# Layer 1's mask row added by VectorE instead of TensorE, and the turned activations y made one step earlier in banks A0 and A1

## The chip, the cores and the metric

The kernel runs on one core of one Trainium2 chip. The metric is the device time of one execution in microseconds (us); of the kernel before, three executions were timed. TensorE (PE in the profile) multiplies matrices and writes PSUM; VectorE (DVE), ScalarE (ACT) and GpSimd (POOL) do the elementwise work; SyncE (SP) issues all the DMAs, in one queue, in program order. Every engine executes its own instructions in order and waits on semaphores where the program says so.

## The reference

Two transformer layers, one after the other, on x of 128 sequences x 64 tokens x 256 features, float32, 16 heads of 16, a hidden layer of 1024. The reference masks layer 1's scores by the given mask.

```
layer 0:  y = LN(x) * (1 + gamma1) + beta1        # one scale and shift per sequence
          x = x + alpha1 * (attention(y) @ proj + b)
          z = LN(x) * (1 + gamma2) + beta2
          x = x + alpha2 * (gelu(z @ fc1 + b1) @ fc2 + b2)
layer 1:  y = LN(x) * (1 + scale1) + shift1
          q, k = rotary(y @ wq + bq), rotary(y @ wk + bk);  v = y @ wv + bv
          scores = where(mask, q.k / 4, -inf);  x = x + softmax(scores) @ v @ wo + bo
          z = LN(x) * (1 + scale2) + shift2
          x = x + gelu(z @ w1 + b1) @ w2 + b2
```

## The kernel before

The tokens are cut into 16 tiles of 512 (8 sequences, four pairs g = 0 to 3 of 128 tokens). Tiles 0 to 15 are layer 0, tiles 16 to 31 the same tokens in layer 1. Every engine has a function `step(u, n, a, b, c, p)` that is written out by hand: step u does the attention of tile u (argument b, its layer), the feed-forward part of tile u-1 (c), the queries, keys and values of tile u+1 (a), the load and first normalisation of tile u+2 (n), and the last additions and the store of tile u-2 (p). Steps 2 to 12 and 18 to 29 are hardware loops, the others are written out. The order of the lines in `step` is each engine's order; nothing reorders them.

Float32 products are made of parts: each operand is split into a high part (float32r) and what is left, and TensorE makes three products of each (`product`, line 977). PSUM has eight banks: A0, A1 (scores, queries and keys), B0, B1 (turned probabilities, their product with the values, values), C (hidden layer), D0, D1 (its second product), E (turned z, heads, projection).

The scores of pair g are two units, (g, b) with b = 0 in A0 and b = 1 in A1. `scores` (L1091) makes a unit in six products. In layer 1 two more follow (L1096): `mean_w`, a matrix of 1/128, times the tile's mask row `mrow` (0 or -2^100) adds the row to all 128 rows of the bank. VectorE's `maximum` (L1444) takes the maximum per head from PSUM, and `subtract` (L1450) writes scores minus maximum to `exps` in SBUF. ScalarE's `exponential` (L804) follows, TensorE's `turn_probs` (L1110) turns the probabilities into B, ScalarE's `move_probs` (L809) copies them out, `weigh_values` (L1124) multiplies them with the values, and VectorE's `reciprocals` and `normalise_heads` (L1460, L1468) divide. `turn_heads` (L1135), `high_heads` (L815, ACT), `low_heads` (L1477, DVE) and `project` (L977 into E) make the projection; `residual` (L1493) adds it to x.

The first normalisation of tile u+2 is `first_statistics` and `first_aggregate` (DVE, L1367 and L1372, wait for the load of `x_in`), `first_rstd` (POOL, L572 to L578), `first_norm` (ACT, L738, in place in x_in) and `first_columns` (ACT, L749, the tile's scales and shifts). One step later `first_turn` (PE, L1031) turns x_in into y, pair 0 in A0 and pair 1 in B1, `y_scale` and `y_shift` (DVE, L1380 and L1387) work on it in PSUM, `first_high` (ACT, L760) and `y_low` (DVE, L1391) write its two parts to SBUF. `queries_keys(i)` for i = 0 to 3 (L977) fills A0, A1, B0, B1. In layer 0 ScalarE's `high_qk` (L776) and VectorE's `low_qk` (L1416) take them; in layer 1 VectorE's `sine` and `cosine` (L1425), four DMAs per chunk that swap partitions, GpSimd's `rotated` (L633), ScalarE's `high_qk` (L780) and GpSimd's `rotated_low` (L639).

On SyncE's queue the load of tile u+2 into x_in (L503) stands behind the store of tile u-2 (which waits for VectorE's `output`, L1517) and behind a copy of 512 KB that waits until that store has landed.

ScalarE loads a table (ACT_TABLE_LOAD) before an instruction whose function is not in the one that is loaded: before the first exponential after a gelu, and before the first gelu after an exponential.

Of the kernel before, what the change touches and what calls it, by code (L numbers as in the profile page):

```python
# [66 lines left out]
def build(nc, t, out):  # L67

    ctx = ExitStack()
    with ctx:  # L70
# [79 lines left out]
        mrow = sb("mrow", [P, TILE], F32R)  # L150
        mean_w = sb("mean_w", [P, P], F32R)
# [49 lines left out]
        pe_s, s_max, s_sub, s_exp = sem("pe_s"), sem("s_max"), sem("s_sub"), sem("s_exp")  # L201
# [71 lines left out]
        def y_bank(pair):  # L273
            return (A[0], B[1])[pair]
# [15 lines left out]

        def chunk_taken(tile, layer, i):

            return (qk_lo, upto(tile, 4, i + 1)) if layer == 0 else (rot_cosed, upto(tile - NT, 4, i + 1))
# [4 lines left out]

        NSPREAD = 16 * (NX + NJ)
# [27 lines left out]
        def _(sp):  # L327
# [140 lines left out]
            def step(u, n, a, b, c, p):  # L468
# [42 lines left out]
                if a == 1:  # L511
                    swap(u + 1, 0)
                    swap(u + 1, 1)
                    swap(u + 1, 2)
                    wait_apart(sp, sp_passed, (pe_s, upto(u + 1, 2 * G, 0)))
                    sp.dma_start(mrow[:, :].bitcast(F32), mask_tiles[u + 1 - NT].partition_broadcast(P))\
                      .then_inc(mrow_in, 16)
                    swap(u + 1, 3)
# [28 lines left out]
        def _(pool):  # L547
# [94 lines left out]
            def step(u, n, a, b, c, p):  # L642
# [40 lines left out]
                if n is not None:  # L683
# [9 lines left out]
        def _(act):  # L693
# [63 lines left out]
            def first_high(tile, pair):  # L757
                act.wait_ge(y_aff, upto(tile, 2, pair + 1))
                await_(act, pe_v, upto(tile, 2, 0))
                nc.scalar.copy(pair_of(yb[0], pair), y_bank(pair)[:, :].rearrange("p (c n) -> p c n", c=KC)).then_inc(y_hi, 1)  # L760
# [57 lines left out]
            def step(u, n, a, b, c, p):  # L818
# [40 lines left out]
                if a is not None:  # L859
# [3 lines left out]
                if a is not None:  # L863
# [28 lines left out]
                elif known(u) and u == 0:  # L892
                    high_piece(2, 0, 2)
                if a == 1:
# [59 lines left out]
                if known(u) and u == NT - 2:  # L954
                    act.wait_ge(mod_done, 32)
                if n is not None:
                    first_norm(u + 2)
                    first_columns(u + 2, n)
                if known(u) and u == 0:
# [10 lines left out]
        def _(pe):  # L970
# [32 lines left out]
            def gate_products():  # L1003
# [3 lines left out]
                pe.wait_ge(consts_ready, 2)  # L1007
# [39 lines left out]
            def queries_keys(tile, layer, i, attn):  # L1047
# [6 lines left out]
                elif attn is None:  # L1054
                    pass
                elif i == 1:
                    pe.wait_ge(s_sub, upto(tile - 1, 2 * G, 6))
# [19 lines left out]
            def scores(u, layer, g, b, a):  # L1077
                if b == 0:
                    pe.wait_ge(spread_in[g % 2], upto(u, 2 * NSPREAD, (g // 2 + 1) * NSPREAD))
                    if layer == 1 and g == 0:  # L1080
                        pe.wait_ge(mrow_in, upto(u - NT, 16, 16))
                await_(pe, s_sub, upto(u, 2 * G, 2 * g + b - 1))
# [4 lines left out]
                s = slice((2 * g + b) * S, (2 * g + b + 1) * S)  # L1087
                for c in range(KC):
                    dst = A[b][:, c * 256:(c + 1) * 256]
                    for p, q in BY_WEIGHTS:  # L1090
                        ins = nc.tensor.matmul(dst, qpad[g % 2][:, c, p, b, :, :].rearrange("p x s -> p (x s)"),  # L1091
                                               kpad[g % 2][:, c, q, :, b * S:(b + 1) * S], start=(p, q) == (0, 0),
                                               stop=layer == 0 and (p, q) == BY_WEIGHTS[-1])
# [80 lines left out]
            def step(u, n, a, b, c, p):  # L1174
# [31 lines left out]
                if a is not None:  # L1206
# [18 lines left out]
                if a is not None:  # L1225
# [512 lines left out]
```

## Time and profile before

| What | Before |
|---|---|
| three executions | 1841.35 us median, 1840.35 to 1844.5 |
| profiled execution | 1841.5 us, its span 1839.7 us (from first to last instruction) |
| PE busy over the span | 1784.3 us, 97% |
| DVE, ACT, POOL busy | 1247.0, 1230.2, 852.7 us (68%, 67%, 46%) |
| mean granted TensorE clock | 0.992 of 2.4 GHz |
| a step of layer 0 (472.22 to 527.07) | 54.85 us, PE busy 54.24 |
| a step of layer 1 (1366.25 to 1421.64) | 55.39 us, PE busy 55.20 |

Busy time is the union of an engine's instructions. Successive products overlap in the records, so that the time one costs is the distance of its start from the next one's, not its length. A step is taken from the first score product of one tile to that of the next. All times in rows are us from the start of the span.

### The profile page before, as it was taken

To read this page: it belongs to the slowest core of one execution; us is meant where nothing else is said; L and a number is where in the kernel's file an instruction comes from. 1 tells how busy PE (TensorE), PEld (TensorE's weight loads), DVE (VectorE), ACT (ScalarE), POOL (GpSimd) and SP (SyncE) were. 2 spreads that over 40 slices of the span, in tenths; PEclk is the share of its full clock that TensorE was granted. 3 is DMA by queue.
4 is the path that set the end of the run, shared out by engine and by line. 5 is a ranking of instruction groups with operands and counts; after the bars stand their busy time and mean duration, and the time that the engine had idled before them with its cause. 6 is when DMAs were issued, how large, how long until landed. Compare 5 with 4: busy or idle time off the path is not lost.

```text
span 1839.7 us, 41543 instructions
## 1 busy us (share of the span) xinstructions
PE 1784.3 (97%) x12623; PEld 1634.3 (89%) x12623; DVE 1247.0 (68%) x2985; ACT 1230.2 (67%) x2265; POOL 852.7 (46%) x1036
## 2 busy tenths in 40 slices
PE   7799999999999999999999999999999999999998
PEld 6688999888989888999888999999999999999986
DVE  6777676667676667677677766776766776666751
ACT  4466767766776766677657767666767667767663
POOL 2233433333433433433635566555566555566544
PEclk9899999999999999999999999999999999999999
DMA  6545545444544435554453332333332334342320
GB/s 166 144 113 127 126 91 126 105 111 125 128 99 116 113 104 130 127 140 103 116 152 100 91 107 88 105 102 105 89 109 86 107 99 107 82 114 88 96 72 35
DMA packets 330283, 199.93 MB, mean 109 GB/s; under 512 B 160995, under 2 KB 314597, under 8 KB 330213
## 3 DMA queue, kind: packets, MB, share of 16 engines
q1 hardware_dynamic: 330212, 199.06, 41.0%
q8 instruction: 36, 0.59, 0.1%
q14 instruction: 35, 0.28, 0.1%
HBM read 80.98 MB, written 17.33 MB: 53 GB/s over the span
## 4 chain that ended last, share of the span: by engine, by line
PE 74%; DVE 11%; issue 7%; ACT 2%; SPq 2%; POOL 2%; DMA 1%; DVEq 0%; POOLq 0%; ACTq 0%
PE C L977 17%; PE D L1168 16%; PE B L977 9%; PE B L1124 8%; PE A L1091 6%; PE B L1110 4%; PE A L977 4%; PE E L977 4%; DVE mx L1444 3%; PE A L1096 2%; DVE o_sb L1468 1%; DVE exps L1450 1%; PE E L1135 1%; PE E L1043 1%; DVE z_lo L1391 1%
## 5 line engine op out<-in xcount | busy, mean ns | idle before, releaser
L593 POOL TENSOR_TENSOR h_lo<-hact,h_hi 128x512 fp32r<-128x512 f32 x256 | 331.0, 1293 | 234.9 <-ACT h_hi L800 219.8
L1168 PE MATMUL D<-wgt_hi,h_hi 128*128 128x256 f32 x1024 | 263.4, 290 | 0.0
L1091 PE MATMUL A<-k_pad,q_pad 128*128 128x256 f32 x1536 | 256.1, 293 | 5.7 <-DMA q_pad<-q_flat 2.8
L809 ACT COPY probs_turned<-B 128x512 f32<-128x512 f32 x256 | 149.3, 584 | 167.6 <-PE B L1110 167.5
L1168 PE MATMUL D<-wgt_lo,h_hi 128*128 128x256 f32 x1024 | 255.6, 282 | 0.0
L1124 PE MATMUL B<-v_blocks,probs_turned 128*128 128x68 f32 x2048 | 254.3, 271 | 1.3 <-ACT probs_turned L809 1.3
L1124 PEld LDWEIGHTS B<-v_blocks,probs_turned 128*128 128x128 f32 x2048 | 248.7, 192 | 6.5 <-ACT probs_turned L809 2.3
L795 ACT ACTIVATE hact<-C,b_col 128x512 f32<-128x512 f32 x256 | 175.9, 687 | 83.6 <-PE C L977 81.2
L1444 DVE TENSOR_REDUCE mx<-A 128x8 f32<-128x512 f32 x256 | 174.4, 681 | 68.8 <-PE A L1096 41.2
L1091 PEld LDWEIGHTS A<-k_pad,q_pad 128*128 128x128 f32 x1536 | 211.3, 191 | 9.8 <-DMA q_pad<-q_flat 3.5
L804 ACT ACTIVATE exps<-exps 128x512 f32<-128x512 f32 x256 | 161.6, 632 | 84.7 <-DVE exps L1450 82.3
L1168 PEld LDWEIGHTS D<-wgt_lo,h_hi 128*128 128x128 f32 x1024 | 195.3, 191 | 1.4
L1168 PEld LDWEIGHTS D<-wgt_hi,h_hi 128*128 128x128 f32 x1024 | 194.6, 190 | 2.0 <-ACT h_hi L800 0.4
L583 POOL TENSOR_SCALAR rs<-mv 128x1 f32<-128x1 f32 x128 | 28.7, 224 | 360.9 <-DVE mv L1501 352.0
L1450 DVE TENSOR_TENSOR exps<-A,mx 128x512 f32<-128x512 f32 x256 | 176.1, 688 | 5.9 <-PE B L1110 0.4
L977 PE MATMUL C<-z_hi,wgt_hi 128*128 128x512 f32 x512 | 169.0, 411 | 5.0 <-ACT hact L795 4.5
L1168 PE MATMUL D<-wgt_hi,h_lo 128*128 128x256 f32 x1024 | 166.8, 285 | 4.7 <-POOL h_lo L593 4.5
L1110 PE MATMUL B<-ident,exps 128*128 128x128 f32 x1024 | 155.8, 275 | 7.4 <-DVE rotation L1425 2.7
L800 ACT CAST h_hi<-hact 128x512 fp32r<-128x512 f32 x256 | 159.1, 621 | 4.2
L1468 DVE TENSOR_TENSOR o_sb<-B,rden 64x128 f32<-64x128 f32 x512 | 146.7, 287 | 20.6
L977 PE MATMUL C<-z_hi,wgt_lo 128*128 128x512 f32 x512 | 159.8, 393 | 0.0
L977 PE MATMUL C<-z_lo,wgt_hi 128*128 128x512 f32 x512 | 158.9, 391 | 0.0
(141 smaller groups left out, 3874.5 us busy)
## 6 DMA issues: line engine op xcount, KB each, us to landing
k_pad<-k_flat SPq DMA_DIRECT2D x512, 64.0 KB, 2.1
q_pad<-q_flat SPq DMA_DIRECT2D x256, 128.0 KB, 2.4
gates<-gates SPq DMA_DIRECT2D x64, 256.0 KB, 4.5
x_bias<-x_bias SPq DMA_DIRECT2D x32, 512.0 KB, 3.3
rotation<-rotation SPq DMA_DIRECT2D x256, 64.0 KB, 1.9
x_in<-in_x SPq DMA_DIRECT2D x16, 512.0 KB, 4.5
gates<-gated_bias SPq DMA_DIRECT2D x32, 256.0 KB, 4.7
x_res<-in_x SPq DMA_DIRECT2D x16, 512.0 KB, 4.8
```

The lines of the kernel that those rows point to most:

```text
L593: pool.tensor_tensor(hb[1][:, m % 2, :], hact[:, m % 2, :], hb[0][:, m % 2, :].bitcast(F32), ALU.subtract).then_inc(h_lo, 1)
L795: nc.scalar.activation(hact[:, m % 2, :], C[:, :], ACT.Gelu, bias=b1_col[:, layer, m:m + 1]).then_inc(gelu, 1)
L800: nc.scalar.copy(hb[0][:, m % 2, :], hact[:, m % 2, :]).then_inc(h_hi, 1)
L804: nc.scalar.activation(exps[:, b, :], exps[:, b, :], ACT.Exp, scale=SCORE_SCALE).then_inc(s_exp, 1)
L977: ins = nc.tensor.matmul(dst, l[p], r[q], start=(p, q) == order[0] and n == 0, stop=(p, q) == order[-1] and n == len(pairs) - 1)
L1091: ins = nc.tensor.matmul(dst, qpad[g % 2][:, c, p, b, :, :].rearrange("p x s -> p (x s)"), kpad[g % 2][:, c, q, :, b * S:(b + 1) * S], sta ...
L1110: ins = nc.tensor.transpose(B[b][:, n * P:(n + 1) * P], exps[:, b, n * P:(n + 1) * P], ident[:, :])
L1124: ins = nc.tensor.matmul(B[b][:, n * 68:(n + 1) * 68], pt[:, b, n * P:(n + 1) * P], moving, start=True, stop=True)
L1168: ins = nc.tensor.matmul(Dk[g // 2][:, (g % 2) * D:(g % 2 + 1) * D], hb[p][:, m % 2, g * P:(g + 1) * P], w_slice(q, W_FF2, D, m, 0, D), st ...
L1444: nc.vector.tensor_reduce(mx[:, b, :], A[b][:, :].rearrange("p (h k) -> p h k", k=S), AX.X, ALU.max)\
L1450: nc.vector.tensor_tensor(exps[:, b, :].rearrange("p (h k) -> p h k", k=S), A[b][:, :].rearrange("p (h k) -> p h k", k=S), mx[:, b, :].rea ...
L1468: ins = nc.vector.tensor_tensor(o_sb[p, b, :].rearrange("p (n j d) -> p n j d", n=4, j=2), sums_of(b)[p, :, x, :, 0:HD], rden[p, b, :].rea ...
```

## The change

Layer 1's `scores` ends with the six products; `mean_w` is gone, and `mrow` is plain float32. VectorE gets a new instruction per unit, `mask`: it reads the bank and the mask row and writes the sum to `exps`. `maximum` then reads `exps`, and `subtract` reads and writes `exps`, so that TensorE may fill the bank again after `mask` (`scores_taken`) and not after `subtract`. Layer 0's units are as before.

From step 1 on, y of tile u+2 is turned at the end of step u, behind `turn_probs(u, 3, 1)`, into A0 and A1; `y_scale`, `y_shift`, `first_high` and `y_low` move to the end of the step too, and the next step's first scores wait for `y_low`. `queries_keys(u+1, 0)` moves up to where the turns were. For that, `first_statistics`, `first_aggregate`, `first_rstd`, `first_norm` and `first_columns` move up in the step. SyncE's order stays as it was.

```diff
+            def mask(u, g, b):
+                s = slice((2 * g + b) * S, (2 * g + b + 1) * S)
+                dve.wait_ge(pe_s, upto(u, 2 * G, 2 * g + b + 1))
+                await_(dve, pe_pt, upto(u, 2 * G, 2 * g + b - 1))
+                if b == 0:
+                    dve.wait_ge(mrow_in, upto(u - NT, 16, 16))
+                nc.vector.tensor_tensor(by_head(exps[:, b, :]), by_head(A[b][:, :]),
+                                        mrow[:, s].rearrange("p (o s) -> p o s", o=1).to_broadcast([P, 8, S]),
+                                        ALU.add).then_inc(s_masked, 1)
+
+            def maximum(u, layer, g, b):
+                if layer == 1 and g in MASKED:
+                    mask(u, g, b)
+                    dve.wait_ge(s_masked, upto(u - NT, NMASK, masked_units(g, b)))
+                    src = exps[:, b, :]
...
+                nc.vector.tensor_reduce(mx[:, b, :], by_head(src), AX.X, ALU.max).then_inc(s_max, 1)
...
+            def subtract(u, layer, g, b):
                 dve.wait_ge(s_max, upto(u, 2 * G, 2 * g + b + 1))
+                src = exps[:, b, :] if layer == 1 and g in MASKED else A[b][:, :]
...
             def scores(u, layer, g, b, a):
...
-                await_(pe, s_sub, upto(u, 2 * G, 2 * g + b - 1))
+                if g > 0:
+                    pe.wait_ge(*scores_taken(u, layer, g - 1, b))
...
+                if g == 0 and a is not None and not y_soon(u):
+                    pe.wait_ge(y_lo, upto(u + 1, 2, b + 1))
...
-                    if layer == 1:
-                        row = mrow[:, s].rearrange("p (o s) -> p o s", o=1).to_broadcast([P, NJ, S])
-                        ins = nc.tensor.matmul(dst, mean_w[:, :], row, start=False, stop=True)
...
@@ TensorE's step
-                if a is not None:
+                if a is not None and y_soon(u):
                     first_turn(u + 1, 0, b)
                     first_turn(u + 1, 1, b)
+                elif a is not None:
+                    queries_keys(u + 1, a, 0, b)
...
                     turn_probs(u, 3, 1, a)
+                if n is not None and b is not None:
+                    first_turn(u + 2, 0, n)
+                    first_turn(u + 2, 1, n)
...
@@ ScalarE's step, behind hidden_high(u - 1, 3)
+                if n is not None and b is not None and a == 0:
+                    first_norm(u + 2)
+                    first_columns(u + 2, n)
...
@@ ScalarE's step, behind exponential(u, 3, 1)
+                if n is not None and b is not None and a == 1:
+                    first_norm(u + 2)
+                    first_columns(u + 2, n)
...
@@ VectorE's step
+                if n is not None and b is not None:
+                    first_statistics(u + 2)
                 if a == 0:
                     low_qk(u + 1, 0)
...
+                if n is not None and b is not None and a == 0:
+                    first_aggregate(u + 2)
                 if a == 0:
                     low_qk(u + 1, 1)
```

VectorE at the start of a step of layer 1 (the loop of steps 18 to 29), before. E is the bank of the turned z, A0 and A1 hold the scores:

```order
L1444 TENSOR_REDUCE mx<-A0 128x8
L1380 TENSOR_TENSOR E<-E,mod_tile 128x512
L1450 TENSOR_TENSOR exps<-A0,mx 128x512
L1444 TENSOR_REDUCE mx<-A1 128x8
L1387 TENSOR_TENSOR E<-E,mod_tile 128x512
L1450 TENSOR_TENSOR exps<-A1,mx 128x512
```

The same place now:

```order
L1483 TENSOR_TENSOR exps<-A0,mrow 128x512
L1495 TENSOR_REDUCE mx<-exps 128x8
L1412 TENSOR_TENSOR E<-E,mod_tile 128x512
L1502 TENSOR_TENSOR exps<-exps,mx 128x512
L1483 TENSOR_TENSOR exps<-A1,mrow 128x512
L1495 TENSOR_REDUCE mx<-exps 128x8
L1419 TENSOR_TENSOR E<-E,mod_tile 128x512
L1502 TENSOR_TENSOR exps<-exps,mx 128x512
```

Each unit has one instruction more, and the pieces of z stand between as before.

ScalarE in the middle of a step of layer 0 (the loop of steps 2 to 12), before; h_hi is the hidden layer's high part, exps the unit (3, 0), q_flat chunk 2 of tile u+1:

```order
L800 CAST h_hi<-hact 128x512
L804 ACT_TABLE_LOAD
L804 ACTIVATE exps<-exps 128x512
L776 ACTIVATE q_flat<-B0,qk_bias 128x4x128
L815 ACTIVATE ot_hi<-E,v_bias 128x128 x2
```

The same place now:

```order
L818 CAST h_hi<-hact 128x512
L756 ACTIVATE x_in<-x_in,nb1,rs1 128x256 x4
L767 COPY mod_tile<-mod 128x32
L822 ACT_TABLE_LOAD
L822 ACTIVATE exps<-exps 128x512
```

The normalisation of tile u+2 now stands ahead of the table load and of the exponential of (3, 0).

VectorE in the middle of a step of layer 1, before; A0 and A1 hold chunks 0 and 1 of tile u+1's keys, B0 the weighed values of unit (2, 0):

```order
L1501 BN_AGGR mv2<-st2 128x2
L1425 SCALAR_TENSOR_TENSOR rotation<-A0,qk_bias,rtab 128x512
L1425 SCALAR_TENSOR_TENSOR rotation<-A0,qk_bias,rtab 128x512
L1425 SCALAR_TENSOR_TENSOR rotation<-A1,qk_bias,rtab 128x512 x2
L1460 RECIPROCAL rden<-B0 128x8
```

The same place now:

```order
L1552 BN_AGGR mv2<-st2 128x2
L1399 BN_STATS st1<-x_in 128x6 x4
L1457 SCALAR_TENSOR_TENSOR rotation<-A0,qk_bias,rtab 128x512
L1457 SCALAR_TENSOR_TENSOR rotation<-A0,qk_bias,rtab 128x512
L1404 BN_AGGR mv1<-st1 128x2 x4
L1457 SCALAR_TENSOR_TENSOR rotation<-A1,qk_bias,rtab 128x512 x2
L1511 RECIPROCAL rden<-B0 128x8
```

The statistics of x_in, which wait for its load, now stand ahead of the first chunk's rotation; they stood some twenty instructions later.

## Rows read from the trace of the kernel before

**Rows 1.** Busy us of PE, PEld, DVE, ACT, POOL, clock, DMA by stretch.

```profile
1366.25:1421.64 55.39, 55.20 (x401) 51.37 (x400) 38.01 (x90) 37.96 (x72) 31.77 (x39) 1.00 0.35 99
1366.25:1384.20 17.95, 17.95 (x151) 17.54 (x150) 15.99 (x34) 12.22 (x23) 8.11 (x8) 1.00 0.35 88
```

**Rows 2.** TensorE's timeline, unit (2, 1): start us, us, engine line op, [idle before].

```profile
1379.44 0.28 PE L1096 MATMUL A<-mrow,mean_w 128*128 128x256 f32 x1
1379.56 0.51 PE L1091 MATMUL A<-k_pad,q_pad 128*128 128x256 f32 x3
```

**Rows 3.** VectorE's timeline, unit (2, 1) and low_heads(0), same step.

```profile
1380.28 0.68 DVE L1444 TENSOR_REDUCE mx<-A 128x8 f32<-128x512 f32 x1
1380.99 0.69 DVE L1450 TENSOR_TENSOR exps<-A,mx 128x512 f32<-128x512 f32 x1
1381.60 0.60 DVE L1477 SCALAR_TENSOR_TENSOR ot_lo<-E,v_bias,ot_hi 128x128 fp32r<-128x128 f32 x2
```

**Rows 4.** TensorE's timeline, project(0) and the turns of y, same step.

```profile
1382.52 0.40 PE L977 MATMUL E<-wgt_hi,ot_hi 128*128 128x256 f32 x2
...
1383.24 0.60 PE L1031 MATMUL A<-ident,x_in 128*128 128x128 f32 x4
1383.78 0.63 PE L1031 MATMUL B<-ident,x_in 128*128 128x128 f32 x4
```

**Rows 5.** Instructions of line L1305: ns min/median/max, first and last start.

```profile
L1305 DVE TENSOR_TENSOR wgt_lo<-gates,wgt_hi x4: 685/686/715, 969.6 to 1004.3; 128x512 fp32r<-128x512 f32 x4
```

**Rows 6.** VectorE's timeline at 965 us, two subtractions between SBUF tensors.

```profile
965.32 3.28 DVE L1305 TENSOR_TENSOR wgt_lo<-w_raw,wgt_hi 128x512 fp32r<-128x512 f32 x2
```

**Rows 7.** Load of x_in, layer 1 step: SyncE's timeline; us to landing.

```profile
1390.81 0.39 SPq L503 DMA_DIRECT2D x_in<-mid  x1
...
x_in<-mid SPq DMA_DIRECT2D x1, 512.0 KB, 4.1
```

**Rows 8.** Timelines of DVE, ACT and PE, same step: chunk 0, turn_probs(3, 0).

```profile
1392.86 1.41 DVE L1425 SCALAR_TENSOR_TENSOR rotation<-A,qk_bias,rtab 128x512 f32<-128x512 f32 x2 [1.41 <-PE A L977]
...
1398.90 0.62 ACT L780 CAST k_flat<-rotation 128x512 fp32r<-128x512 f32 x1 [1.30 <-POOL rotation L633]
...
1404.43 0.60 PE L1110 MATMUL B<-ident,exps 128*128 128x128 f32 x4
```

**Rows 9.** Load of x_in, layer 0 step: SyncE's timeline; us to landing.

```profile
496.93 0.39 SPq L503 DMA_DIRECT2D x_in<-in_x  x1
...
x_in<-in_x SPq DMA_DIRECT2D x1, 512.0 KB, 4.7
```

**Rows 10.** Timelines of DVE and POOL, layer 0 step: statistics and rstd of x_in.

```profile
515.31 1.37 DVE L1367 BATCH_NORM_STATS2 st<-x_in 128x6 f32<-128x256 f32 x4
516.95 0.38 DVE L1372 BATCH_NORM_AGGREGATE mv<-st 128x2 f32<-128x6 f32 x4 [0.27 <-DVE st L1367]
...
518.42 0.23 POOL L572 TENSOR_SCALAR rs<-mv 128x4 f32<-128x4 f32 x1
...
520.26 0.24 POOL L578 TENSOR_SCALAR nb<-nb 128x4 f32<-128x4 f32 x1 [0.20 <-POOL nb L576]
```

**Rows 11.** Groups by line, whole span: xcount | busy us, mean ns | idle before.

```profile
L738 ACT ACTIVATE x_in<-x_in,nb,rs 128x256 f32<-128x256 f32 x128 | 66.4, 590 | 9.1 <-POOL nb L578 9.1
```

**Rows 12.** Timelines of ACT, DVE and PE, layer 0 step: up to turn_probs(3, 0).

```profile
503.70 1.28 ACT L804 ACT_TABLE_LOAD   x1
507.85 0.63 ACT L804 ACTIVATE exps<-exps 128x512 f32<-128x512 f32 x1 [2.87 <-DVE exps L1450]
...
509.09 0.75 DVE L1416 SCALAR_TENSOR_TENSOR q_flat<-B,qk_bias,q_flat 128x512 fp32r<-128x512 f32 x1 [1.27 <-ACT q_flat L776]
...
509.98 0.65 PE L1110 MATMUL B<-ident,exps 128*128 128x128 f32 x4
```

**Rows 13.** Columns as in rows 1 (the clock last but two), at a long wait.

```profile
951.40:954.80 3.40, 1.18 (x8) 0.78 (x7) 0.75 (x1) 1.89 (x2) 3.28 (x3) 1.00 0.10 36
954.80:961.60 6.80, 5.47 (x21) 4.92 (x21) 4.28 (x8) 5.20 (x10) 4.20 (x4) 0.50 0.17 59
```

More of the change, by code:

```diff
@@ L271, in qk_bank, with y_soon, y_bank @@
             return (A + B)[i]
-        def y_bank(pair):
-            return (A[0], B[1])[pair]
+        def y_soon(u):
+            return known(u) and u < 1
+        def y_bank(tile, pair):
+            return (A[0], B[1] if known(tile) and tile < 2 else A[1])[pair]
         def pair_of(buf, pair):
@@ L289, in head_rows, with masked_units, scores_taken @@
             return E[:, 0:2 * P].rearrange("p (b x q) -> p b x q", b=2, x=NX)[:, :, x, :]
+        def masked_units(g, b):
+            return 2 * sum(m < g for m in MASKED) + (b + 1 if g in MASKED else 0)
+        def scores_taken(tile, layer, g, b):
+            if layer == 1 and g in MASKED:
+                return s_masked, upto(tile - NT, NMASK, masked_units(g, b))
+            return s_sub, upto(tile, 2 * G, 2 * g + b + 1)
         def chunk_taken(tile, layer, i):
@@ L682, in step @@
                     rotated_low(u + 1, 3)
-                if n is not None:
+                if n is not None and b is None:
                     first_rstd(u + 2)
@@ L862, in step @@
                     second_norm(u, 0)
[L863 removed]
+                if y_soon(u):
                     first_high(u + 1, 1)
@@ L1224, in step @@
                     modulations(Dk[0], ada_raw[0][:, :, D:2 * D], ada_raw[0][:, :, 0:D])
-                if a is not None:
+                if a is not None and y_soon(u):
                     queries_keys(u + 1, a, 0, b)
@@ L1587, in step @@
                     gate_heads(u, 1)
-                if a is not None:
+                if y_soon(u):
                     y_shift(u + 1, 1)
@@ L1593, in step @@
                     residual(u, b, 1)
-                if a is not None:
+                if y_soon(u):
                     y_low(u + 1, 0)
@@ L1620, in step @@
                     low_piece(3, 0, 3)
+                if n is not None and b is not None:
+                    first_statistics(u + 2)
                 if a == 0:
@@ L1631, in step @@
                     cosine(u + 1, 0)
+                if n is not None and b is not None and a == 1:
+                    first_aggregate(u + 2)
+                if a == 1:
                     sine(u + 1, 1)
@@ L1665, in step @@
                     second_aggregate(u, 2)
-                if n is not None:
+                if n is not None and b is None:
                     first_statistics(u + 2)
                     first_aggregate(u + 2)
+                elif n is not None:
+                    for pair in range(2):
+                        y_scale(u + 2, pair)
+                        y_shift(u + 2, pair)
                 if known(u) and u == NT - 2:
@@ L1694, in step @@
                     second_aggregate(u, 3)
+                if n is not None and b is not None:
+                    y_low(u + 2, 0)
+                    y_low(u + 2, 1)
                 if known(u) and u == NT - 1:
```

108 lines of the change are left out of this document (57 added, 51 removed).

## The prediction

> **What bounds it now.** The busy times of the whole span put TensorE at 97% (the table above). I then looked at single steps. A step of layer 1 takes 55.39 us and TensorE is busy in 55.20 of them [rows 1]: it hardly waits, so a us of work taken from it is a us gained, and a us of new waiting is a us lost, since the rest of its step has no holes to make it up. The second row cuts off the part up to turn_heads(1): there VectorE is busy 15.99 of 17.95 us, and 38.01 - 15.99 = 22.0 in the 37.4 us behind it. So VectorE, at 69% over the step, is nearly full in one part of it, and the change puts six of its eight new instructions there. The third view is the timeline, engine by engine, around the places where something is moved.
>
> **What TensorE sheds.** One mask product starts at 1379.44 and the next score product at 1379.56 [rows 2]: 0.12 us. Two per unit, 8 units, 16 tiles make 256, or 30.7 us.
>
> **What VectorE takes on.** No row shows a mask addition. The nearest are the maximum and the subtraction of the same 128x512: 0.68 and 0.69 us, 0.71 from start to start where the second needs the first, 0.61 where the next does not [rows 3]. The maximum needs the mask, so I take 0.71 of the two. Reading SBUF instead of PSUM gains nothing for the maximum and the subtraction: a 128x512 subtraction between SBUF tensors takes 0.686 us [rows 5], against 0.69 [rows 3]. The Trainium skill's page "VectorE: DVE Perf Modes", section "The TRN2 errata", counts 58 cycles beside the elements for an SBUF source and 120 for a PSUM source, which would be an estimated 0.065 us less for each of the twelve before project(0), 0.8 us a step; the trace does not agree with it ([rows 3, 5]), and the sum goes by the rows.
>
> Another price is a collision. Two subtractions with both inputs in SBUF took 3.28 us together [rows 6] instead of 1.37 [rows 5], 0.96 more each, while GpSimd worked beside them. The new subtraction has both inputs in SBUF (exps and mx); the old one had one in PSUM and took 0.69. For each subtraction the bounds are 0 (mx has only 8 elements a row) and 0.96. GpSimd is busy 8.11 of the first 17.95 us, in 8 instructions [rows 1], which I expect mostly at the start of the step: I take one collision of 0.55, near the middle; bounds 0 and 6 x 0.96 = 5.8. The Trainium skill's page "SBUF — State Buffer", section "Who interferes with whom", says that a VectorE instruction with two SBUF inputs and a GpSimd instruction that reads SBUF exclude each other for the whole instruction. The trace agrees for two full inputs [rows 6]; that an input as small as mx is enough, no row here shows.
>
> **Where it ends first: project(0).** Six units stand ahead of low_heads(0) on VectorE: 6 x 0.71 = 4.26, less 0.24 because the first scores are two products sooner, plus 0.55: 4.6. low_heads(0) ended at 1381.60 + 0.60 = 1382.2 [rows 3] and would end at 1386.8. project(0), which needs it, started at 1382.52 [rows 4]: 4.3 late (3.7 without the collision), where TensorE by itself would come 6 x 0.24 = 1.4 early. What is queued behind it on TensorE's queue is all the rest of the step.
>
> **The load of x_in, layer 1.** The change moves the statistics of tile u+2 far up VectorE's order but leaves the load where it was, behind the store of tile u-2 and a copy. It is issued at 1390.81 and lands 4.1 later [rows 7], at 1394.9. The store waits for VectorE's output behind low_heads(1), which the 4.3 us shift: 1399.2. VectorE now waits there ahead of chunk 0's rotation, which started at 1392.86 [rows 8]. Statistics 1.37 [rows 10]: the rotation starts at 1400.6. From its start to the end of ScalarE's cast of the chunk it is 1398.90 + 0.62 - 1392.86 = 6.66 us [rows 8] (sine, four DMAs, GpSimd): 1407.2. On ScalarE a table load of 1.28 and the exponential of (3, 0), 0.63, follow [rows 12]: 1409.1, and then turn_probs(3, 0), which was at 1404.43 [rows 8]: 4.7 late. Behind it come the turns of y, now at the end of the step: two groups 0.54 apart [rows 4], 1.1 us. The last unit's mask and a collision of its subtraction stand ahead of low_heads(2) and project(2): between 0 and 1.2, I take 0.6. A step is 4.7 + 1.1 + 0.6 = 6.4 longer; steps 16 to 29, 14 x 6.4 = 90. Steps 30 and 31 load no x_in; there the 4.3 are lessened by the products behind project(0) and, in step 30, by the turns of y: 3.0 and 3.8, 7 in all.
>
> **The same in layer 0.** No masks here, but x_in is issued at 496.93 and lands 4.7 later [rows 9], 501.6. Statistics 1.37, low_qk(0) 0.75 [rows 10, 12], aggregates 0.38: 504.1. GpSimd's rstd, 520.26 + 0.24 - 518.42 = 2.08 [rows 10]: 506.2. Four normalisations, 66.4 / 32 = 2.08 [rows 11]: 508.3. The table load was over at 504.98, in 2.87 us of idle time that hid it [rows 12]; the order has it behind the normalisations now, 1.28: 509.6. So the exponential of (3, 0) starts 1.75 after 507.85, and with it high_qk(2), low_qk(2) and turn_probs(3, 0), which was at 509.98 right behind low_qk(2) (509.09 + 0.75) [rows 12]. TensorE's turns of y are gone ahead of this place, but a chain that starts with a DMA sets it, so they are gained nowhere and cost 1.1 behind it. 2.85 a step; 15 steps (1 to 15) make 42.
>
> **TensorE's clock.** Around 951 TensorE was busy 1.18 of 3.40 us, and the next 6.8 us were granted 0.50 [rows 13], 1.2 GHz, which loses 3.4 us of work. The new waits are of that size (about 5.7 us before project(0), in several pieces; 2 to 3 before turn_probs(3, 0)). Bounds: none, and 3.4 in each of 29 steps, 99. As the waits come in pieces between work I take one step in six: 16.
>
> **At nothing.** The next step's scores wait for y_low at the end of the step; TensorE's back(5) and hidden(7) stand there and should cover it. Without that cover it would be one more 0.7 instruction a step, 20 us. The mask row's load waits for the last mask now, ahead of swap 3 on SyncE's queue; swap 3 waits for a later instruction of VectorE's anyway.
>
> **Sum.** The shorter products are within the lines above. 42 + 90 + 7 + 16 = 155 us on the profiled execution's 1841.5, which stands at the median of 1841.35: 1996 us.
>
> **Rivals.** (1) Ends on the other side: the masks are hidden and TensorE's 30.7 us come through: 1811. For it, TensorE's full row [rows 1]; against it, project(0) had 0.3 us of room (1382.2 to 1382.52) and 4.6 come in. It decides at an addition of 0.05 us a unit. Chance 0.03. (2) x_in lands in time and only the masks tell: 4.3 less the 0.5 of the last units' products, 3.8 in 16 steps: 1902. It needs a landing ahead of about 500 in layer 0, that is a load issued 2 us sooner; the waits ahead of it on SyncE's queue are not changed, but a shorter transfer is possible. 0.15. (3) The masks fit better than I think (VectorE slips into waits), x_in is late: layer 0's 42 alone, since in layer 1 a chain that starts 1.4 us earlier gives back what the turns of y cost: 1884. 0.06. (4) The clock falls in every step, and collisions add to it: 1980 + 99 = 2079, half of it 2030. For it [rows 13] and the length of the waits; 0.17. My forecast has 0.58; 0.01 is left for no change.
>
> **Range.** The likeliest case by itself: 1950 to 2030 (x_in half a us earlier or later moves all 29 steps, 15 us; collisions 0 or 1 us more in 14 steps, the clock 0 to 50). To hold 8 in 10 it must reach (2) and a good part of (4): 1885 to 2060. A change under 0.2%, 3.7 us, could not be told from none by these runs. Slower by more 0.96, within 0.01, faster 0.03.
>
> **What would show it.** Steps of layer 0 near 57.7 us, with an ACT_TABLE_LOAD between the normalisation of x_in and the exponential, and VectorE idle some 6 us ahead of L1399 with the DMA as releaser. Steps of layer 1 near 62 us; project(0) waiting some 2 us for VectorE's ot_lo, more pieces of waiting for ScalarE's exponentials and copies before it; VectorE's first rotation behind the statistics. Subtractions (L1502) of up to 1.6 us beside GpSimd. The granted clock below 0.99. Wrong would be: layer 0 steps of 55 us (x_in came sooner, or something else was ready later), or a layer 1 step under 58.

## The result, and the profile after

The changed kernel takes 2043.88 us (median of 6 executions, 2032.9 to 2051.47) against 1842.81 us of the kernel before, run beside it (6 executions, 1840.35 to 1844.5): a ratio of 1.1088, 95% interval 1.1065 to 1.1111, so 11% slower. The prediction had 1996 us; the loss is about 201 us where 155 were forecast. The profiled execution took 2038.69 us, its span 2036.8.

The head of its page:

```profile
span 2036.8 us, 41383 instructions
...
PE 1822.0 (89%) x12367; PEld 1638.4 (80%) x12367; DVE 1381.8 (68%) x3112; ACT 1243.1 (61%) x2265; POOL 872.2 (43%) x1036
```

TensorE was full before (97%) and now has 11% of holes; its busy time is even 38 us longer than before although 256 products are gone; the granted clock is lower (0.971 after 0.992). Stretch by stretch, with the columns of [rows 1]: a step of layer 1, its part up to turn_heads(1), a step of layer 0, two more of layer 0, and step 0:

```profile
1494.35:1558.68 64.33, 55.24 (x386) 49.46 (x384) 46.13 (x99) 38.46 (x70) 33.21 (x38) 1.00 0.30 86
1494.35:1517.29 22.94, 18.30 (x138) 16.46 (x136) 20.64 (x41) 12.81 (x20) 8.96 (x7) 1.00 0.27 69
...
383.36:442.37 59.01, 55.74 (x386) 50.51 (x384) 38.12 (x93) 38.59 (x70) 20.76 (x27) 0.97 0.43 107
442.37:499.99 57.62, 54.42 (x385) 49.33 (x384) 38.12 (x93) 38.63 (x70) 20.77 (x27) 1.00 0.43 109
...
32.66:94.77 62.11, 42.79 (x273) 38.84 (x273) 44.04 (x116) 29.55 (x62) 8.37 (x17) 0.89 0.53 135
```

Against [rows 1]: the layer 1 step went from 55.39 to 64.33 us, and its first part from 17.95 to 22.94, of which VectorE is busy 20.64. A step of layer 0 takes 57.6 us at a granted clock of 1.00 (54.85 before), 59.0 where the clock fell for a while (0.97), and step 0, which holds no feed-forward work, grew from 54.2 to 62.1.

Where TensorE waits in that layer 1 step (its timeline; the last column is the idle time ahead of the row and who ended it):

```profile
1499.56 0.66 PE L1138 MATMUL B<-ident,exps 128*128 128x128 f32 x4 [1.04 <-ACT exps L822]
1502.09 0.66 PE L1138 MATMUL B<-ident,exps 128*128 128x128 f32 x4 [1.15 <-ACT exps L822]
1506.88 0.65 PE L1138 MATMUL B<-ident,exps 128*128 128x128 f32 x4 [0.39 <-DVE o_sb L1519]
1515.11 0.47 PE L1004 MATMUL E<-wgt_hi,ot_hi 128*128 128x256 f32 x2 [2.06 <-DVE ot_lo L1528]
1533.03 0.73 PE L1004 MATMUL B<-y_hi,wgt_hi 128*128 128x512 f32 x2 [1.10 <-DVE o_sb L1519]
1539.04 0.65 PE L1138 MATMUL B<-ident,exps 128*128 128x128 f32 x4 [1.80 <-DVE rotation L1457]
1542.58 0.47 PE L1004 MATMUL E<-wgt_hi,ot_hi 128*128 128x256 f32 x2 [1.49 <-DVE ot_lo L1528]
```

The first four are the delay ahead of project(0), in pieces (4.6 us of idle time), which now starts 20.76 us into the step and not 16.27 [rows 4]. The other three (4.4 us) come behind the late x_in in the step; two of them have a second cause, which the experiments below show. On VectorE in the same step:

```profile
1497.39 1.46 DVE L1502 TENSOR_TENSOR exps<-exps,mx 128x512 f32<-128x512 f32 x1
1498.77 0.68 DVE L1483 TENSOR_TENSOR exps<-A,mrow 128x512 f32<-128x512 f32 x1
...
1527.87 1.41 DVE L1399 BATCH_NORM_STATS2 st<-x_in 128x6 f32<-128x256 f32 x4 [6.11 <-DMA x_in<-mid]
1529.19 1.39 DVE L1457 SCALAR_TENSOR_TENSOR rotation<-A,qk_bias,rtab 128x512 f32<-128x512 f32 x2
...
1535.38 1.61 DVE L1502 TENSOR_TENSOR exps<-exps,mx 128x512 f32<-128x512 f32 x1
1536.92 0.74 DVE L1457 SCALAR_TENSOR_TENSOR rotation<-B,qk_bias,rtab 128x512 f32<-128x512 f32 x1
1538.16 0.75 DVE L1457 SCALAR_TENSOR_TENSOR rotation<-B,qk_bias,rtab 128x512 f32<-128x512 f32 x1 [0.51 <-POOL k_flat L655]
...
1540.26 1.65 DVE L1502 TENSOR_TENSOR exps<-exps,mx 128x512 f32<-128x512 f32 x1
```

and on GpSimd beside them:

```profile
1495.90 2.40 POOL L624 TENSOR_TENSOR x_bias<-x_res,b_bc 128x1024 f32<-128x1024 f32 x1
...
1535.16 1.29 POOL L609 TENSOR_TENSOR h_lo<-hact,h_hi 128x512 fp32r<-128x512 f32 x1
1536.41 1.72 POOL L655 TENSOR_TENSOR k_flat<-rotation,k_flat 128x512 fp32r<-128x512 f32 x1
...
1540.08 1.29 POOL L655 TENSOR_TENSOR k_flat<-rotation,k_flat 128x512 fp32r<-128x512 f32 x1 [0.73 <-ACT k_flat L798]
```

Two things are to be seen. VectorE stands idle for 6.11 us until x_in lands, with chunk 0's rotation right behind the statistics. And three subtractions take 1.46, 1.61 and 1.65 us: each ends 0.54 to 0.55 us after the GpSimd instruction that was running when it began (1495.90 + 2.40 = 1498.30, and 1497.39 + 1.46 = 1498.85; likewise 1536.45 and 1536.99, 1541.37 and 1541.91). In turn the GpSimd instruction that starts under a subtraction is stretched, to 1.72 us in place of 1.29. The mask at 1498.77, which takes one input from PSUM, runs beside GpSimd in its 0.68.

The load (SyncE's timeline, then us to landing), which answers to [rows 7]:

```profile
1523.85 0.39 SPq L519 DMA_DIRECT2D x_in<-mid  x1
...
x_in<-mid SPq DMA_DIRECT2D x1, 512.0 KB, 4.0
```

Issued 29.50 us into the step, 24.56 before. In the layer 0 step that begins at 499.99, on VectorE, ScalarE and TensorE:

```profile
529.64 1.41 DVE L1399 BATCH_NORM_STATS2 st<-x_in 128x6 f32<-128x256 f32 x4 [6.80 <-DMA x_in<-in_x]
...
534.37 2.08 ACT L756 ACTIVATE x_in<-x_in,nb,rs 128x256 f32<-128x256 f32 x4 [4.49 <-POOL nb L594]
536.58 1.28 ACT L822 ACT_TABLE_LOAD   x1
537.87 0.63 ACT L822 ACTIVATE exps<-exps 128x512 f32<-128x512 f32 x1
...
539.99 0.65 PE L1138 MATMUL B<-ident,exps 128*128 128x128 f32 x4 [2.47 <-DVE q_flat L1448]
```

This step takes 57.97 us. It shows the chain that was forecast: landing, statistics, rstd, four normalisations, a table load that nothing hides any more, exponential, and turn_probs(3, 0) behind it, 40.00 us into the step and not 37.76 [rows 12].

### The profile page after: what moved, and what is told of

Same layout as the page of the kernel before. It is cut to its first block, busy times and chain, and to the rows that moved or that the text cites. A ratio compares the mean times of both kernels' runs of the same rounds, so it can differ in the third digit from the quotient of the medians.

```text
span 2036.8 us, 41383 instructions
## 1 busy us (share of the span) xinstructions
PE 1822.0 (89%) x12367; PEld 1638.4 (80%) x12367; DVE 1381.8 (68%) x3112; ACT 1243.1 (61%) x2265; POOL 872.2 (43%) x1036
## 4 chain that ended last, share of the span: by engine, by line
PE 36%; DVE 27%; issue 15%; DMA 12%; POOL 4%; ACT 3%; SPq 3%; DVEq 1%; POOLq 0%; ACTq 0%
PE C L1004 10%; PE B L1004 6%; PE D L1196 6%; DVE mx L1495 5%; DVE exps L1502 4%; DMA x_in<-in_x 4%; PE E L1004 3%; PE B L1152 3%; DVE exps L1483 3%; DMA x_in<-mid 3%; DMA mid<-x_bias 3%; DVE o_sb L1519 2%; DVE ot_lo L1528 2%; DMA out<-x_bias 2%; PE B L1138 2%
## 5 line engine op out<-in xcount | busy, mean ns | idle before, releaser
L609 POOL TENSOR_TENSOR h_lo<-hact,h_hi 128x512 fp32r<-128x512 f32 x256 | 339.6, 1326 | 281.0 <-ACT h_hi L818 270.9
L1196 PE MATMUL D<-wgt_hi,h_hi 128*128 128x256 f32 x1024 | 269.8, 295 | 0.0
L1152 PE MATMUL B<-v_blocks,probs_turned 128*128 128x68 f32 x2048 | 263.1, 277 | 1.5 <-ACT probs_turned L827 1.5
L1152 PEld LDWEIGHTS B<-v_blocks,probs_turned 128*128 128x128 f32 x2048 | 254.2, 197 | 11.1 <-ACT probs_turned L827 5.3
L1196 PE MATMUL D<-wgt_lo,h_hi 128*128 128x256 f32 x1024 | 261.1, 287 | 0.0
L1122 PE MATMUL A<-k_pad,q_pad 128*128 128x256 f32 x1536 | 245.7, 297 | 12.8 <-DVE k_flat L1448 4.3
L1138 PE MATMUL B<-ident,exps 128*128 128x128 f32 x1024 | 161.9, 282 | 91.3 <-ACT exps L822 36.3
L1122 PEld LDWEIGHTS A<-k_pad,q_pad 128*128 128x128 f32 x1536 | 205.5, 194 | 19.3 <-issue 9.9
L1138 PEld LDWEIGHTS B<-ident,exps 128*128 128x128 f32 x1024 | 121.0, 145 | 120.1 <-issue 71.1
L1399 DVE BATCH_NORM_STATS2 st<-x_in 128x6 f32<-128x256 f32 x128 | 45.0, 413 | 188.3 <-DMA x_in<-mid 99.9
```

Source lines behind the costliest of these rows:

```text
L609: pool.tensor_tensor(hb[1][:, m % 2, :], hact[:, m % 2, :], hb[0][:, m % 2, :].bitcast(F32), ALU.subtract).then_inc(h_lo, 1)
L1138: ins = nc.tensor.transpose(B[b][:, n * P:(n + 1) * P], exps[:, b, n * P:(n + 1) * P], ident[:, :])
L1152: ins = nc.tensor.matmul(B[b][:, n * 68:(n + 1) * 68], pt[:, b, n * P:(n + 1) * P], moving, start=True, stop=True)
L1196: ins = nc.tensor.matmul(Dk[g // 2][:, (g % 2) * D:(g % 2 + 1) * D], hb[p][:, m % 2, g * P:(g + 1) * P], w_slice(q, W_FF2, D, m, 0, D), st ...
```

## The experiments

The theory after the result: x_in, still loaded where it was, holds VectorE up in every step; in layer 1 the masks delay project(0), and the subtraction in SBUF collides with GpSimd. The rivals: that x_in is a bystander, that ScalarE's new order sets layer 0, that the masks would fit by themselves. Every kernel is given against the kernel before, run on the same chip; in brackets stand the ratio of the two and its 95% interval. Differences between experiments are differences of medians, some of them from two chips; on these chips the kernel before took 1841.84 to 1843.01 us.

**x_in sooner.** The load stands behind the spreads of group 3:

```diff
                     spread_queries(u, 3)
+                if n is not None and x_soon(u, b):
+                    wait_apart(sp, sp_passed, (pe_yt, upto(u + 1, 2, 2)))
...
+                    sp.dma_start(x_in, tokens_of(u + 2, n)).then_inc(x_loaded, 16)
```

> Against the changed kernel, only the load of x_in is moved: from behind the store of tile u-2 and the copy to right behind the spreads of group 3 of the same step. My theory: the landing of x_in sets the middle of every step. Then VectorE's 6.1 us of idle time ahead of the statistics is gone, layer 0 steps go from about 57.5 us to 54.9 to 55.8, and layer 1 steps from 64.5 to 60 to 62 (project(0) still comes 4.8 late), so about 40 + 14 x 3.5 = 90 us less than the changed kernel's 2044: 1955 (1935 to 1980). Rival: the load is a bystander, the masks and collisions in layer 1 and the normalisation and table load on ScalarE in layer 0 set the steps anyway; then at most 0.5 us a step is gained: over 2025.

Measured: 1939.71 us (1.0521, 1.0489 to 1.0553), 104 us less than the changed kernel. One step of either layer (columns of rows 1):

```profile
474.47:528.77 54.30, 54.11 (x385) 49.22 (x384) 38.39 (x93) 38.64 (x70) 20.78 (x27) 1.00 0.48 116
1411.24:1472.63 61.39, 56.06 (x386) 50.87 (x384) 45.63 (x99) 38.39 (x70) 32.14 (x38) 0.97 0.31 90
```

The time lies in the range given, and the load does set both layers: layer 0 loses all of its 2.75 us and 0.5 more, layer 1 loses 3 of its 9. In layer 1 TensorE still waits 0.87 us for turn_probs(3, 0) and 0.78 us for project(2) (1.80 and 1.49 in the changed kernel), and for project(0). What remains there is due to the masks, as the next experiments show.

**The same, with x_in's normalisation later on ScalarE** (x_in_norm_later: in layer 0 behind the exponential of (3, 1) too).

```diff
-                if n is not None and b is not None and a == 0:
-                    first_norm(u + 2)
-                    first_columns(u + 2, n)
...
-                if n is not None and b is not None and a == 1:
+                if n is not None and b is not None:
                     first_norm(u + 2)
```

> As x_in_sooner, and in layer 0 the four normalisations of x_in on ScalarE stand behind the exponential of (3, 1), as they do in layer 1, so that the table load ahead of the exponential of (3, 0) has its idle time back. My theory: with x_in in time the normalisations come early enough either way, so the same time as x_in_sooner within 8 us, layer 0 steps near 55.0 us. Rival: ScalarE's order was the cause in layer 0 (2.75 us a step); then this run is 30 to 45 us faster than x_in_sooner.

Measured: 1951.35 us (1.0584, 1.0562 to 1.0607), 12 us slower than x_in sooner, where its expectation allowed 8; layer 0 steps of 54.83 against 54.30. Layer 1 is the same program in both. A step of each layer:

```profile
480.05:534.88 54.83, 54.37 (x386) 49.19 (x384) 38.51 (x93) 38.28 (x70) 20.77 (x27) 1.00 0.47 115
1485.93:1547.03 61.10, 54.78 (x385) 49.33 (x384) 45.37 (x99) 38.45 (x70) 32.64 (x38) 1.00 0.32 90
```

The rival (30 to 45 us faster) falls: ScalarE's order is no burden when x_in is in time, and the place that the change chose is the better one. About half of the 0.5 us stands in the trace: TensorE waits 0.27 us for VectorE's q_flat ahead of turn_probs(3, 1), a wait that x_in sooner does not have. The rest was not followed up.

**The normalisation later, x_in late.** The same edit in the changed kernel itself.

> The changed kernel with x_in's load as late as there, but in layer 0 the four normalisations of x_in on ScalarE stand behind the exponential of (3, 1) instead of ahead of the table load and the exponential of (3, 0). My theory, by the prediction's chain in layer 0: landing, statistics, aggregates, rstd, normalisations 2.08, table load 1.28, exponential, high_qk(2), low_qk(2), turn_probs(3, 0); without the normalisations and the table load in it the exponential is in time and layer 0 steps fall from about 57.5 to 58.5 us to 55 to 56: 2044 - 30 = 2014 (2005 to 2025), layer 1 as in the changed kernel. Rival: the late statistics hold VectorE up by themselves (low_qk(0) and all behind it) and the normalisations lie in ScalarE's waits: layer 0 steps of 57 and more, 2035 to 2050.

Measured: 2022.15 us (1.0974, 1.0951 to 1.0997), 22 us less than the changed kernel and in the range given; a layer 0 step, a little longer than the 55 to 56 us expected, and the row of turn_probs(3, 0) in it:

```profile
493.21:549.50 56.29, 54.71 (x386) 49.31 (x385) 38.25 (x93) 38.32 (x70) 20.82 (x27) 1.00 0.45 112
```

```profile
531.02 0.65 PE L1135 MATMUL B<-ident,exps 128*128 128x128 f32 x4 [0.46 <-DVE q_flat L1445]
```

The wait fell from 2.47 to 0.46: the normalisations and the exposed table load were part of the chain, as the prediction had it, and about half of layer 0's loss (1.3 us of 2.75 by these rows, 22 / 15 = 1.5 on average). The other half, 1.4 us against the kernel before, remains with the statistics still late; with the same order on ScalarE and the load in time a step took 54.83 us (x_in_norm_later). So both halves come from the one late load.

**y alone.** The mask products are back on TensorE (`MASKED = ()`, `mean_w` as before), y stays one step sooner.

> The changed kernel with the mask products back on TensorE and no mask on VectorE in any unit; y stays one step sooner. My theory: layer 0 as in the changed kernel (about 57.5 to 58.5 us a step, 50 us in all); in layer 1 project(0) is in time, x_in lands as before about 29 us into the step, the statistics hold chunk 0's rotation up by 3.7 us, of which 1.7 were slack: steps of 57.5 to 59.5. In all 1842 + 50 + 14 x 3 = 1934 (1915 to 1955). Rival: the move of y costs in layer 0 only, and layer 1 is slow by the masks alone: layer 1 steps of 55.4 to 56, 1892.

Measured: 1918.2 us (1.0408, 1.039 to 1.0425), in the range given; steps of 57.83 in layer 0 and 57.63 in layer 1, so that y costs in both layers and the rival falls:

```profile
497.18:555.01 57.83, 54.48 (x385) 49.37 (x384) 38.13 (x93) 38.65 (x70) 20.79 (x27) 1.00 0.44 109
1430.36:1487.99 57.63, 55.41 (x401) 51.19 (x400) 38.30 (x91) 38.18 (x70) 31.73 (x38) 1.00 0.33 96
```

**The masks alone.** y, x_in and the statistics as before.

> The kernel before with the masks on VectorE and no mask products, and y, x_in and their statistics where they stood before. Layer 0 is the kernel before, 54.8 us a step. My theory: project(0) waits 4.8 us longer for low_heads(0), the masks and the long subtractions of (3, 0) and (3, 1) add 1 to 2: layer 1 steps of 59.5 to 61.5, 1842 + 16 x 5.1 = 1924 (1905 to 1945). Rival: the masks are mostly hidden when nothing else is moved, and the late x_in made layer 1 slow: layer 1 steps of 54 to 56.5, 1820 to 1860.

Measured: 1948.42 us (1.0579, 1.0559 to 1.0599), 3 us above the range given. A layer 1 step, and project(0) in it:

```profile
1417.57:1478.68 61.11, 54.96 (x386) 49.38 (x384) 44.72 (x98) 38.31 (x71) 32.68 (x39) 1.00 0.31 90
```

```profile
1438.54 0.47 PE L1004 MATMUL E<-wgt_hi,ot_hi 128*128 128x256 f32 x2 [2.05 <-DVE ot_lo L1528]
```

The masks cost 105 us and y 75, together 181 of the 201. The rest fits with the two lengthening each other's chain: the masks shift the store that x_in's load waits for, and y hangs on that load, which is issued 24.94 us into a layer 1 step with y alone and 29.50 with both. That this makes the whole 20 us is not shown. Masks that would be hidden if nothing else moved fall as a theory.

**The masks in PSUM.** From x_in sooner, without the collision: the sum is written back to the bank, and maximum and subtraction read the bank again.

```diff
-                nc.vector.tensor_tensor(by_head(exps[:, b, :]), by_head(A[b][:, :]),
+                nc.vector.tensor_tensor(by_head(A[b][:, :]), by_head(A[b][:, :]),
                                         mrow[:, s]...
...
-                src = exps[:, b, :] if layer == 1 and g in MASKED else A[b][:, :]
+                src = A[b][:, :]
```

> As x_in_sooner, but VectorE adds the mask row in place in PSUM: maximum and subtraction read the PSUM bank again, so no subtraction has both inputs in SBUF; the bank is released at the subtraction instead of at the mask. My theory: in x_in_sooner's trace a subtraction that runs beside GpSimd ends 0.54 us after GpSimd's instruction does, and takes 1.46, 1.48 and 0.94 us in place of 0.69 (units (0, 0), (3, 0), (3, 1)); here all take 0.69 and no GpSimd instruction is stretched to 1.73; project(0) waits 0.6 us less and turn_probs(3, 0) and project(2) lose most of their 0.87 and 0.78 us of waiting: layer 1 steps of 59.2 to 60.2 instead of 61.4, 1939 - 14 x 1.7 = 1915 (1905 to 1923). Rival: the masks' own 0.7 us each set the steps and the collisions lie in waits: within 8 us of x_in_sooner; or the later release makes the next scores wait and it is slower than x_in_sooner.

Measured: 1914.99 us (1.041, 1.0391 to 1.043), 24.7 us less than x_in sooner by the medians (20 by the two ratios). The subtractions, ns min/median/max: first the changed kernel's two forms, then this kernel's:

```profile
L1502 DVE TENSOR_TENSOR exps<-A,mx x128: 678/691/694, 35.0 to 950.2; 128x512 f32<-128x512 f32 x128
L1502 DVE TENSOR_TENSOR exps<-exps,mx x128: 680/692/2377, 970.5 to 1984.1; 128x512 f32<-128x512 f32 x128
```

```profile
L1506 DVE TENSOR_TENSOR exps<-A,mx x256: 675/691/693, 34.9 to 1855.8; 128x512 f32<-128x512 f32 x128
```

A layer 1 step at a granted clock of 1.00, to be held against the 61.10 above:

```profile
1336.54:1395.84 59.30, 54.77 (x385) 49.38 (x384) 43.64 (x99) 38.48 (x70) 31.67 (x38) 1.00 0.32 93
```

With one input in PSUM none takes more than 0.693 us; with both in SBUF the longest took 2.377. In this step no GpSimd addition or subtraction of 128x512 takes more than 1.30 us, turn_probs(3, 0) no longer waits, and project(2) waits 0.55. So the collision is shown, and it costs 20 to 25 us in 16 steps, 1.3 to 1.5 each (1.8 by the two rows at a granted 1.00). This is a net price: the bank now comes free only at the subtraction, and the next scores wait for it in places (0.25 and 1.12 us in this step). project(0) waits all the same (2.09 us; steps of 59.3 to 60.9): that is the masks' own time.

**x_in sooner and y, no masks on VectorE.** x_in sooner with `MASKED = ()`.

> As x_in_sooner with the mask products back on TensorE and no mask on VectorE: y one step sooner and the load of x_in in time. My theory: layer 0 as in x_in_sooner (54.3 us a step); in layer 1 the waits that y_alone still has (0.89 and 1.33 us) go with the late x_in: TensorE full, 54.6 to 55.2 us a step against 55.4; step 0 still some 6 us over. In all 1842 - 8 - 7 + 6 = 1833 (1825 to 1845), faster than the kernel before by 0 to 1 per cent. Rival: layer 1's rotation chain is late by the statistics ahead of it in any case: 56 to 57.5 us a step, 1850 to 1870.

Measured: 1829.11 us (0.9931, 0.9914 to 0.9947), in the range given and faster than the kernel before by 0.7%:

```profile
473.18:527.50 54.32, 54.18 (x385) 49.28 (x384) 38.38 (x93) 38.64 (x70) 20.75 (x27) 1.00 0.48 116
1357.48:1412.42 54.94, 54.94 (x402) 51.25 (x400) 38.43 (x91) 38.16 (x70) 31.69 (x38) 1.00 0.35 100
```

Both layers gain half a us a step. In layer 0 part of it is a wait of the kernel before (TensorE's timeline, turn_heads(1), which waited behind the turns of y for VectorE's residual); with the longer queries_keys(0) in the turns' place it is covered:

```profile
490.09 0.44 PE L1135 MATMUL E<-ident,o_sb 128*128 128x128 f32 x2 [0.29 <-DVE x_res L1493]
```

**The last mask on VectorE.** As x_in_y with `MASKED = (3,)`, in SBUF and, in a second kernel, in PSUM.

> As x_in_y, but VectorE adds the mask for group 3 alone (two units a step, in SBUF as in the changed kernel), TensorE multiplies it for groups 0 to 2. My theory: ahead of project(0) VectorE is full, so masks cost there what they take; behind it, where the statistics no longer wait, it has room, and the mask of group 3 costs only its collisions with GpSimd (0.8 and 0.25 us): layer 1 steps of 54.8 to 56, 1828 to 1850. Rival: a mask costs its 0.7 us at any place: 56 us or more a step, 1850 to 1865.

> As mask_last, with the mask added in place in PSUM. My theory: no collision is left and the two masks fit: 0.48 us a step less on TensorE than x_in_y, 54.2 to 54.8 us a step in layer 1, 4 to 8 us faster than x_in_y and 5 to 15 faster than mask_last: 1820 to 1835. Rival: as for mask_last, the same time as mask_last within 3 us.

Measured: 1854.32 us in SBUF (1.0066, 1.0049 to 1.0083) and 1839.66 us in PSUM (0.9987, 0.9977 to 0.9997), both above the ranges given (1828 to 1850, 1820 to 1835). In SBUF, TensorE waits in a step for turn_probs(3, 0) and project(2):

```profile
1410.33 0.65 PE L1154 MATMUL B<-ident,exps 128*128 128x128 f32 x4 [0.86 <-DVE rotation L1474]
1413.15 0.47 PE L1013 MATMUL E<-wgt_hi,ot_hi 128*128 128x256 f32 x2 [0.78 <-DVE ot_lo L1545]
```

and in PSUM for project(2) alone:

```profile
1400.55 0.47 PE L1011 MATMUL E<-wgt_hi,ot_hi 128*128 128x256 f32 x2 [0.54 <-DVE ot_lo L1541]
```

The collision costs 14.7 us here too. It is part of why the SBUF kernel came out where its rival had put it (1850 to 1865). But the expectation that two masks fit behind project(0) was wrong as well: in PSUM they still cost 10.6 us against x_in_y, and low_heads(2) stands behind them.

**low_heads(2) first**, and a kernel that also moves the last modulations of step 0 behind y_low.

```diff
+                if b == 1:
+                    low_heads(u, b, 2)
                 if b is not None:
                     maximum(u, b, 3, 1)
                     subtract(u, b, 3, 1)
+                if b == 0:
                     low_heads(u, b, 2)
```

> As mask_last_psum, and in layer 1 low_heads(2) stands ahead of the mask, maximum and subtraction of (3, 1) on VectorE. My theory: the one wait of mask_last_psum in layer 1, 0.54 us of project(2) for ot_lo, is gone, and the 0.48 us of mask products come through: 54.3 to 54.6 us a step in layer 1 against 54.92 of x_in_y: 1822 (1815 to 1830), faster than x_in_y by 3 to 10. Rival: the exponential of (3, 1) is 2 us later and turn_probs(3, 1) waits for it instead: 55 to 55.6 us a step, no faster than x_in_y's 1829.

> As heads_first, and in step 0 VectorE's last twelve modulation instructions (layer 1, second norm) stand at the end of the step, behind y_low, instead of ahead of the last normalisations. My theory: step 0 (60 us, 54.2 in the kernel before) waits 3.58 us for turn_heads(3) and 2.44 us for y_low; both fall by about 2.3 us: 2 to 5 us less than heads_first. Rival: the modulations only move into step 1, which is as much longer: the same as heads_first within 1.5 us.

Measured: 1828.04 us (0.9925, 0.9909 to 0.9941) and 1829.07 us (0.9931, 0.9915 to 0.9947).

```profile
1354.25:1409.02 54.77, 54.69 (x397) 50.78 (x396) 39.69 (x93) 38.09 (x70) 31.87 (x38) 1.00 0.35 101
```

The wait is gone, 11.6 us less than mask_last_psum. But of the 0.48 us of products only some 0.2 come through (54.77 after 54.94, where 54.3 to 54.6 was expected), so it is level with x_in_y; no wait of TensorE shows in either step, and where the rest went is open. The second edit shortens step 0 from 59.01 to 56.25 us and lengthens step 1 from 55.34 to 58.37: its rival held. heads_first, heads_mods and x_in_y are level, and all three beat the kernel before by 0.7%.

## Why the prediction was right, and where it was too small

The time lies in the range given, and above the narrower 1950 to 2030 of the likeliest case. Here it is taken apart by the prediction's own terms, in the span (2036.8 - 1839.7 = 197 us more). Steps 1, 16 and 30 and the end lie at 86.48, 913.63, 1698.74 and 1839.71 before, at 94.77, 967.63, 1884.03 and 2036.76 after.

| Term | Predicted | Measured |
|---|---|---|
| layer 0, steps 1 to 15 | 42 (15 x 2.85 is nearer 43) | 15 x 2.75 = 41 |
| layer 1, steps 16 to 29 | 90 | 14 x 8.94 = 125 |
| steps 30, 31 | 7 | 12 |
| clock | 16 | no more than what is left of steps 1 to 29 (177 - 41 - 125): 11 |
| step 0 | 0 | 8 |

**Right** (forecast, and in brackets measured). Masks of 0.71 us (0.68 to 0.69, 0.71 to the maximum behind it); reading SBUF is no cheaper for the maximum (0.686 from SBUF, 0.681 from PSUM); project(0) late by 4.3 (4.5), and by 3.7 without the collision (3.7 in masks_in_psum, 19.97 us into its step after 16.27). x_in's load was taken to be late by the same 4.3 (4.9), and the rotation behind it by 7.7 (8.2). In layer 0 the statistics' start was forecast at 29.4 us into the step and came at 29.65, and the exponential of (3, 0) came 0.5 later than forecast. The sum came out: in the step of 57.62 us turn_probs(3, 0) starts 1.9 us later than before (1.75 forecast), and what stands behind it takes 0.9 us more (1.1 forecast).

Rival 2 (the masks alone tell, 1902) fails twice: x_in was not in time, and when an experiment brought it in time the kernel still took 1940, since the masks by themselves cost 5.7 us a step (61.11 in mask_alone) and not 3.8. Rivals 1 and 3, with the masks hidden, fall with mask_alone. Rival 4 (the clock falls in every step and collisions add; half of it 2030) is in part what happened: its collisions came, but not its price for the clock (below).

Layer 1's 8.94 us a step against the 6.4 forecast are 6.5 before turn_probs(3, 0) (4.7 forecast), 1.7 from there to project(2) (0.6) and 0.7 behind that (1.1).

**Mis-sized: the collisions in layer 1.** "I take one collision of 0.55" and "the last unit's mask and a collision of its subtraction ... between 0 and 1.2, I take 0.6" are the terms. There are three collisions a step, of 0.77, 0.92 and 0.96, and mx, with 8 elements a row, locks GpSimd out as a full input does. The upper bound of 0.96 each holds for these three, and the value taken was too near the lower one; one subtraction in step 16 went past the bound, 2.38 us beside a GpSimd instruction of 2.39. By the two experiments with and without them the collisions cost 20 to 25 us. From turn_probs(3, 0) to project(2) it was 1.83 us before, 1404.43 [rows 8] to 1406.26:

```profile
1406.26 0.40 PE L977 MATMUL E<-wgt_hi,ot_hi 128*128 128x256 f32 x2
```

and is now 3.54 (1539.04 to 1542.58): 1.7 more where 0.6 was taken and 1.2 was the bound.

**Mis-sized: what turn_probs(3, 0) waits for.** 4.7 us late was forecast, from the exponential; it is 6.5 late. The exponential ended at 1537.16 + 0.63 = 1537.79, 0.6 us later in the step than forecast:

```profile
1537.16 0.63 ACT L822 ACTIVATE exps<-exps 128x512 f32<-128x512 f32 x1
```

But what TensorE waited for, until 1539.04, was chunk 2's second rotation, which has to read bank B before the turn writes there. VectorE reached it late behind the stretched subtraction, and it then waited 0.51 us for GpSimd's stretched rotated_low. That is the collision a second time, on both engines: with the last masks in SBUF this turn waits 0.86 us (mask_last), with them in PSUM not at all (mask_last_psum).

**Left out: step 0**, 8 us. It has no feed-forward work to cover anything. The new place of y starts with this step, and not with step 1 as the part on the change says: step 0 turns y of tile 1 in the old place and y of tile 2 at its end. There the wait for y_low, which the prediction put at nothing because back(5) and hidden(7) would cover it, has no such cover, and step 1's first scores wait 2.44 us:

```profile
94.77 1.46 PE L1122 MATMUL A<-k_pad,q_pad 128*128 128x256 f32 x6 [2.44 <-DVE y_lo L1423]
```

In the later steps TensorE shows no such wait. The load of x_in in step 0 stood behind layer 1's weights, and TensorE waited 2.37 us for turn_probs(3, 0) there too.

**The clock** was forecast at one fall of 3.4 us in six steps. Falls were more frequent and cost less each: 21 of steps 1 to 29 have a granted clock under 1.00, but in steps 3 to 15 those at 1.00 take 57.2 to 58.0 us and those at 0.97 take 58.4 to 59.4. Against a full-clock step in every place, steps 1 to 29 together are 25 us longer, where the kernel before had 14; the difference is the 11 of the table. How much of it is the clock's alone is not shown.

## What to carry to other kernels

When an instruction is moved ahead, move the transfer that it waits for as well: the queue of the engine that issues it has an order of its own, and in this case one load in an unchanged place cost 104 of 201 us. An operation moved onto an engine that is 69% busy on average costs nearly its full time where that engine is full just then (six masks of 0.71 us put project(0) back by 3.7 us without any collision); look at the stretch ahead of the next consumer, not at the mean. If VectorE and GpSimd work at the same time, keep one input of VectorE's two-input instructions in PSUM where it already lies there (20 to 25 us here).

## What was not expected of the hardware

A subtraction with both inputs in SBUF is shut out, though the second has only 8 elements a row, for the whole of a GpSimd instruction, 1.65 us in place of 0.69, and a GpSimd instruction that starts under it waits in turn (1.72 in place of 1.29). The Trainium skill's page "SBUF — State Buffer", section "Who interferes with whom", says that a VectorE instruction with two SBUF inputs contends with a GpSimd instruction that reads SBUF; the trace agrees, for a small input too, and the same subtraction with one input in PSUM never took more than 0.694 us. The Trainium skill's page "VectorE: DVE Perf Modes", section "The TRN2 errata", would have an SBUF source cost less than one in PSUM by its table's cycles; the trace does not agree for a 128x512 maximum, 0.686 us from SBUF and 0.681 from PSUM (medians):

```profile
L1495 DVE TENSOR_REDUCE mx<-A x128: 639/681/693, 34.3 to 949.5; 128x8 f32<-128x512 f32 x128
L1495 DVE TENSOR_REDUCE mx<-exps x128: 685/686/689, 969.3 to 1983.4; 128x8 f32<-128x512 f32 x128
```
